# Each transfer by index waits for the last but one before it to land: sort, layers 0, 2, 3 and last stage of a four-layer graph network

## What is computed

```python
# layer 0, two steps: gated messages
edge_feat = concat([h[src], h[dst]]); messages = mlp(edge_feat) * sigmoid(mlp_att(edge_feat))
h = mlp(concat([h, segment_sum(messages, dst)])) + h + global_repr
# layer 1: segment_sum(x[col], row), then linear, batch norm, relu, linear
# layer 2: typed attention, 8 heads
attn = einsum('ehd,ehd->eh', Q[edge_dst], K[edge_src]) * rel_scale[edge_rel] / sqrt(DH)
out = segment_sum(softmax_over_dst(attn)[..., None] * V[edge_src], edge_dst) @ Wo + bo + skip
# layer 3: scores from q[src], k[tgt], edge attributes, distances; softmax over tgt
attended = weights[..., None] * v[tgt]; out = segment_sum(attended, tgt) @ Wo + bo
```

## Time and profile before

| | us |
|---|---|
| median of three timed runs (lowest, highest) | 7089.4 (7088.25, 7090.32) |
| span of the profiled execution | 8961.2 |
| its mean granted TensorE clock, share of full speed | 0.674 |
| PE busy in it | 5673.7 |
| DVE busy in it | 4867.9 |
| POOL busy in it | 4865.9 |

### The profile page before, as it was taken

One profiled execution on the slowest core, in us unless ns is written; L12 is line 12 of the kernel. 1 busy time (PEld: TensorE's weight loads), 2 busy tenths in 40 slices (PEclk: granted clock), 3 DMA queues, 4 the chain that ended last, 5 costly groups with the idle time before them and its releaser, 6 DMA issues. The chain is left out here.

```text
span 8961.2 us, 134318 instructions
## 1 busy us (share of the span) xinstructions
PE 5673.7 (63%) x28658; PEld 4800.1 (54%) x28659; DVE 4867.9 (54%) x17338; ACT 1151.3 (13%) x3238; POOL 4865.9 (54%) x4715
## 2 busy tenths in 40 slices
PE   6555556677777767777768778656666665333334
PEld 5555555466666556666655555456666663333333
DVE  6555554455555545555557777545555553444555
ACT  1111111111111111111112222100000001000001
POOL 2566564555555355555527888445454451566664
PEclk6555555777777877777779999865655556555556
DMA  5334434333333233333324444333333332333332
GB/s 154 95 95 97 94 94 126 92 97 93 95 93 96 57 102 94 94 97 98 94 53 67 69 69 69 78 83 88 89 89 87 89 89 37 77 75 75 74 77 49
DMA packets 930244, 770.85 MB, mean 86 GB/s; under 512 B 586631, under 2 KB 762899, under 8 KB 928115
## 3 DMA queue, kind: packets, MB, share of 16 engines
q0 software_dynamic: 245936, 426.87, 19.9%
q1 hardware_dynamic: 675276, 329.60, 14.6%
q10 hardware_dynamic: 8960, 13.52, 0.6%
HBM read 681.88 MB, written 86.32 MB: 86 GB/s over the span
## 5 line engine op out<-in xcount | busy, mean ns | idle before, releaser
L1180 POOL DMA_INDIRECT there<-table_wide,idx x1664 | 1597.4, 960 | 1396.8 <-DVE prod L1203 615.9
L1271 PE MATMUL ps<-here,hot_t 128*128 x3328 | 1238.1, 507 | 631.3 <-DVE there L1222 599.7
L2288 POOL DMA_INDIRECT there<-table_wide,idx x832 | 792.7, 953 | 902.6 <-DVE msg L2364 434.8
L1222 DVE TENSOR_TENSOR there<-there,ps 128x512 f32<-128x512 f32 x832 | 571.2, 687 | 1169.8 <-remote 607.7
L1271 PEld LDWEIGHTS ps<-here,hot_t 128*128 128x128 f32 x3328 | 740.9, 247 | 756.5 <-issue 668.9
L2677 POOL DMA_INDIRECT there<-table_narrow,idx x832 | 791.3, 951 | 649.5 <-issue 259.1
L693 POOL DMA_INDIRECT rec<-out_recd,posd x806 | 817.5, 1014 | 564.4 <-issue 263.9
L1279 PE MATMUL ps<-relu,hot_s 128*128 128x128 f32 x3328 | 878.0, 356 | 140.3 <-DVE hot_s L1211 108.1
L2837 PE MATMUL ps<-here,hot_t 128*128 x1664 | 434.5, 436 | 803.6 <-DVE prod L2758 419.3
L1947 POOL DMA_INDIRECT partial_sums<-row_sums1a,idx1a x504 | 814.9, 1617 | 167.4 <-issue 147.3
L1279 PEld LDWEIGHTS ps<-relu,hot_s 128*128 128x128 f32 x3328 | 688.5, 238 | 326.3 <-issue 272.1
(11 more groups left out here) (486 smaller groups left out, 9773.3 us busy)
## 6 DMA issues: line engine op xcount, KB each, us to landing
locrows<-loc_row SPq DMA_DIRECT2D x416, 256.0 KB
krowd<-key_row SPq DMA_DIRECT2D x201, 256.0 KB
there<-table_wide,idx POOLq DMA_INDIRECT x2496
src_rows1a<-slot_src_row SPq DMA_DIRECT2D x42, 768.0 KB
lrowd<-lo_row SPq DMA_DIRECT2D x201, 128.0 KB
attr_raw<-in_edge_attr SPq DMA_DIRECT2D x201, 128.0 KB
there<-table_narrow,idx POOLq DMA_INDIRECT x832
rec<-out_recd,posd POOLq DMA_INDIRECT x806
```

The source lines that it names most:

```text
L1180: nc.gpsimd.indirect_dma_start(there[:, j, q, :], None, table, bass.IndirectOffsetOnAxis(idx[:, j, q:q + 1], 0)).then_inc(gathered[j][q], 16)
L1222: nc.vector.tensor_tensor(pair, pair, ps[:, WORK, :], ALU.add).then_inc(summed, 1)
L1271: last = nc.tensor.matmul(ps[:, WORK, (q % 2) * 2 * F:(q % 2 + 1) * 2 * F], hot_t[:, j % 2, q * P:(q + 1) * P], here[:, :, :].rearrange("p ...
L2288: nc.gpsimd.indirect_dma_start(there[:, j, q, :], None, table, bass.IndirectOffsetOnAxis(idx[:, j, q:q + 1], 0)).then_inc(gathered[j][q], 16)
```

## The change

Before each gather or scatter by index, from the third on, Pool waits until the one two before it has landed, then increments `admitted`; after each group it waits for the landing of the group's last but one. At the second of a group the gathers of layers 0, 2 and 3 wait for the last of the group before. In the last stage the single semaphore `found` becomes two in turn, and DVE waits for both. Nothing is computed otherwise.

```diff
--- before.py
+++ after.py
@@ -690,8 +690,12 @@
                     pool.wait_ge(kept, i * 4 + (j + 3))
                     pool.sem_inc(admitted, 1)
                     for g in range(n):
+                        if g >= 2:
+                            pool.wait_ge(sent[j][g - 2], i * 16 + 16)
+                        pool.sem_inc(admitted, 1)
                         nc.gpsimd.indirect_dma_start(rec, bass.IndirectOffsetOnAxis(pos[:, j, g:g + 1], 0),
                                                      out[:, j, g, :], None).then_inc(sent[j][g], 16)
+                    pool.wait_ge(sent[j][n - 2], i * 16 + 16)
 
                 with pool.Fori(0, QUADS) as i:
                     for j in range(SLOTS):
@@ -1177,8 +1181,14 @@
                             pool.wait_ge(cut, i * RING * PR + (j * PR + q // 2 + 1))
                         pool.wait_ge(dotted, i * CH + (j * U + q + 1))
                         pool.sem_inc(admitted, 1)
+                        if q >= 2:
+                            pool.wait_ge(gathered[j][q - 2], i * 16 + 16)
+                        elif q == 1 and j:
+                            pool.wait_ge(gathered[j - 1][U - 1], i * 16 + 16)
+                        pool.sem_inc(admitted, 1)
                         nc.gpsimd.indirect_dma_start(there[:, j, q, :], None, table,
                                                      bass.IndirectOffsetOnAxis(idx[:, j, q:q + 1], 0)).then_inc(gathered[j][q], 16)
+                    pool.wait_ge(gathered[j][U - 2], i * 16 + 16)
 
         @block.vector
         def _(dve):
@@ -2920,10 +2942,11 @@
         turned, weight_kept, weight_made = c.sem("wo_turned"), c.sem("wo_kept"), c.sem("wo_centred")
         v_made, v_kept, moved, cen_made, cen_kept = c.sem("v_made"), c.sem("v_kept"), c.sem("h_moved"), c.sem("hc_made"), c.sem("hc_kept")
         ends_turned, line_step, lifted, spread = c.sem("ends_turned"), c.sem("line_steps"), c.sem("line_lifted"), c.sem("carry_spread")
-        found, node_step, node_lifted, massed = c.sem("runs_found"), c.sem("node_steps"), c.sem("node_lifted"), c.sem("massed")
+        node_step, node_lifted, massed = c.sem("node_steps"), c.sem("node_lifted"), c.sem("massed")
         weighed, agg_turned, agg_kept, projected = c.sem("weighed3"), c.sem("agg_turned3"), c.sem("agg_kept3"), c.sem("projected3")
         centred, squared, var_ready, rooted = c.sem("centred_last"), c.sem("squared_last"), c.sem("var_last"), c.sem("rooted_last")
         inverted, returned, normed, finished = c.sem("inverted_last"), c.sem("returned_last"), c.sem("normed_last"), c.sem("finished_last")
+        paced, founds = c.sem("paced_last"), [c.sem(f"runs_found{n}") for n in range(2)]
         out_turned, out_kept, stored = c.sem("out_turned3"), c.sem("out_kept3"), c.sem("out_stored")
         block = ctx.enter_context(nc.Block())
         SP = len(SPANS)
@@ -2932,8 +2955,12 @@
         @block.gpsimd
         def _(pool):
             for t in range(NB):
-                nc.gpsimd.indirect_dma_start(found_rows[:, t, :], None, spool, bass.IndirectOffsetOnAxis(run["pos"][:, t:t + 1], 0)).then_inc(found, 16)
-            pool.wait_ge(found, 16 * NB)
+                if t >= 2:
+                    pool.wait_ge(founds[t % 2], 16 * (t // 2))
+                pool.sem_inc(paced, 1)
+                nc.gpsimd.indirect_dma_start(found_rows[:, t, :], None, spool, bass.IndirectOffsetOnAxis(run["pos"][:, t:t + 1], 0)).then_inc(founds[t % 2], 16)
+            pool.wait_ge(founds[0], 16 * ((NB + 1) // 2))
+            pool.wait_ge(founds[1], 16 * (NB // 2))
 
         @block.tensor
         def _(pe):
@@ -3027,7 +3054,8 @@
             nc.vector.tensor_tensor(carried_in[:, 0, :, :], carried_in[:, 0, :, :],
                                     run["early"][:, :].rearrange("p (t o) -> p t o", o=1).to_broadcast([P, NB, H]), ALU.min).then_inc(node_step, 1)
             dve.wait_ge(node_step, 5)
-            dve.wait_ge(found, 16 * NB)
+            dve.wait_ge(founds[0], 16 * ((NB + 1) // 2))
+            dve.wait_ge(founds[1], 16 * (NB // 2))
             nc.vector.tensor_tensor(joint[:, :, :], found_rows[:, :, 0:H], carried_in[:, 0, :, :], ALU.max).then_inc(node_step, 1)
             dve.wait_ge(node_step, 6)
             nc.vector.tensor_tensor(scale[:, 0, :, :], found_rows[:, :, 0:H], joint[:, :, :], ALU.subtract).then_inc(node_step, 1)
```

## The result

| | before | after |
|---|---|---|
| median of 4 runs, us (lowest to highest) | 7088.82 (7069.89 to 7090.32) | 9705.5 (9686.01 to 9712.0) |
| span of the profiled execution shown, us | 8961.2 | 9699.9 |

The ratio is 1.3694, 95% interval 1.3672 to 1.3716: slower by 2617 us. Predicted were 8500 us, range 7230 to 8980. The sign was right; the size was not. (In experiment 3 one execution of four took 10761.6 us, at a granted clock of 1.0, where the others took 7627.66 to 7637.19; it is left out there.)

A forecast was written before the change was run, and what follows sets the result against it. The prediction took Pool's issue of index transfers as the bound: 4134 x 1.61 = 6656 us, layer 1 968.7, between layer 0's steps 120.0, the rest 747.0 and last stage 9 made 8501, so 8500 us; range 7230 to 8980.

The forecast's parts named there:

- Pool's issue bounds the timed kernel: All five stages with index transfers: Pool's issue, about 1.25 us a transfer back to back, sets the unprofiled pace; chance 0.74.
- Unprofiled, PE and DVE run faster: Reason given: without the profiler PE and DVE free slots in time, so some 1886 us of Pool's profiled idle time vanish.
- The agreement of 7075 with 7089: Sum of Pool's own pace (5239 us), layer 1, the time between layer 0's steps and the rest, against the measured median.
- everything shrinks without the profiler: Rival: the whole profile, Pool included, scales by 0.79 in timed runs, so the change costs about +140: 7230 us; chance 0.12.
- The instructions cost nothing: Added waits and increments on Pool are worked off during the 0.95 us of the transfer before, at no cost.
- D = 0.80 us: Time on Pool from a landing event to the start of the transfer that waited for it, read in layer 2.
- The wait is read ahead: Rival: a landing needs only 0.30 us to the next start, so the pace is 1.37 us, total 7502; chance 0.08.
- L = 2.43 us, with ends 2.2 and 2.65: Time from a transfer's start on Pool to its landing; gives a pace of 1.61 us, with ends 1.50 and 1.725.
- All other terms together: Forecast parts outside the paced transfers: layer 1 968.7 us, between layer 0's steps 120.0, the rest 747.0, last stage 9.
- Pairs and a pace, nothing hidden: Paced stages: interval is half of landing time plus restart delay; each stage lasts count x pace, ring depth hiding no pace.
- A gain by less traffic beside SP's loads: Rival: fewer gathers in flight speed SP's row loads in layers 0 and 2, some 30 to 50 us: 7050; chance 0.03.
- What would show it: Signs: Pool idle 0.5 to 0.8 us before transfers, starts two apart 3.1 to 3.5 us, busy 0.95, timed excess over 400.

The follow-up runs named there:

- experiment 3: The change's waits in layer 2 alone, against the kernel before on the same chip: 7631.14 us, ratio 1.0787.
- Experiment 0: The kernel before, unchanged, measured again on a chip other than that of the 8961.2 us profile: 7084.81 us, ratio 1.0012.
- experiment 1: Kernel before with as many added waits and increments in the sort and layers 0, 2, 3, each on an event long past: 7078.19 us, ratio 0.9999.
- experiment 4: Kernel before with each gather of layer 2 alone waiting for the landing of the one just before: 10477.46 us, ratio 1.169.
- 8: The changed kernel against the kernel before, both on a chip where the latter takes about 8975 us: 9653.51 us, ratio 1.0767.
- experiment 2: Kernel before with each transfer in the sort and layers 0, 2, 3 waiting for the landing of the fourth before it: 7131.45 us, ratio 1.0082.
- experiment 6: Layer 2 paced at two and SP's row-number loads there cut to an eighth, against the kernel before: 8945.27 us, ratio 0.9968.
- experiment 11: Kernel before with each transfer in the sort and layers 0, 2, 3 waiting for the third before it: 8734.01 us, ratio 0.9746.

## Why the prediction was right, and where it failed

- **Pool's issue bounds the timed kernel: right.** Experiment 0 shows the intervals that were computed (1.25 us back to back) and idle time of 0.30 us times the count. **The reason given for it was wrong.** "Unprofiled, PE and DVE run faster" has no ground; the profile shown was of a chip on which they are held up. The agreement of 7075 with 7089 was no accident (the stretches of experiment 0 make 5395 us where 5359 were counted, the rest 1683 where 1716 were), but it said what the bound was, not why the profile differed. The rival *everything shrinks without the profiler* falls with its premise.
- **The instructions cost nothing: right** (experiment 1).
- **D = 0.80 us: nearly right.** The chain of the changed kernel has 0.75; in its events the median is 0.77 in the three gather stages, and the mean, which counts, 0.89 to 0.91. *The wait is read ahead*, at 0.30, is refuted.
- **L = 2.43 us, with ends 2.2 and 2.65: this step failed.** The view of one line of the changed kernel (its median the middle number) and the page's list of DMA issues (median to landing last) have

```profile
DMA to landing us min/median/max: 2.6/2.8/4.9
```

```profile
there<-table_wide,idx POOLq DMA_INDIRECT x2496, 2.8
there<-table_narrow,idx POOLq DMA_INDIRECT x832, 2.5
rec<-out_recd,posd POOLq DMA_INDIRECT x806, 3.1
```

  The shortest landing of layer 2 (first fence, L2303) is 2.6 us, above the value taken. Its mean, by the events, is 3.06, with 2.95 in layer 0, 2.93 in layer 3 and 2.95 in the sort. Two errors make it up. The lower bound of 2.2 was the end of the bytes, read in the earlier trace rows, and the event comes later than they do: 0.35 us in the median over the gathers of experiment 4. And the upper bound of 2.65 was one landing, the last of the run, in a stage whose own landings are shorter: 2.22 to 2.38 us in most of the chain above. A single row was taken for a mean, while the load after the eighth gather had shown 3.19 and was set aside.
- **What it was worth.** The four stages (layer 0 without the 120 us between its steps) last 1515.0 + 3174.8 + 1640.9 + 1593.3 = 7924 us, that is 1.917 a transfer where 1.61 was taken: +1268 us. All other terms together came out 69 us lower than forecast. L + D is 3.83 on the mean instead of 3.23; some 0.5 of the difference is L, the rest D. With 2.95 and 0.88 in the same sum the forecast would have been 4134 x 1.915 + 1845 = 9762.
- **Pairs and a pace, nothing hidden: right.** Experiments 3, 4 and 8 show the interval as (L + D) / 2 in the gather stages, on both kinds of chip, and on A the growth of the four stretches adds up to that of the span within 27 us. In the sort the prediction's own remark counts: no transfer waits for the fourth scatter of a group, which lands latest (3.68 us in the mean, the other three 2.54 to 2.81), so starts two apart are 3.76 us, less than the mean L and D of all would give (4.04).
- **A gain by less traffic beside SP's loads: not on A** (experiment 2 is slower), and seven eighths of the row loads are worth 0.03 us a gather (experiment 6).
- **What would show it.** Idle time ended by its own DMA: yes, but 0.95 to 1.04 us a gather in place of 0.5 to 0.8. Starts two apart: 3.5 to 4.1 in the timeline, 3.8 to 4.0 in the mean, in place of 3.1 to 3.5. Busy 0.955 in layer 0 as foreseen, 1.02 in layer 2. A profiled span of 9000 to 9400: 9699.9 and, on the kind of chip for which it was meant, 9639.7.
- **The Trainium skill**, "DMA: Bandwidth & Descriptors", section "Anatomy of one DMA — SWDGE (gpsimd) path", gives 2.3 us for a transfer of 128 KB, an estimate by that page: for the wide gathers of the changed kernel 0.5 below the median of 2.8, and 0.6 to 0.8 below the mean that counts here. The section "Latency and other measured facts" has the fixed cost fall with a lighter load of HBM; with seven eighths of the row loads gone the median landing of layer 2 is 2.9 us against 3.0 on the same chip (26 landings each), the way the page says, but too small and on too few landings to bear it out.

## What to carry to other kernels

When a queue is limited to n transfers in flight, its pace is (time to landing + time from the event to the next start) / n, and it must be compared with the pace at which the engine issues: here 3.83 / 2 = 1.92 against 1.25 us, while at four the limit costs 0.8%. Take the time to landing as a mean over many transfers of that very stage, from engine start to event, never from the end of the bytes or from one transfer, and look which transfers of a group are late and whether anything waits for them: half a microsecond in it was over 1000 us here. And where a profiled span and the timed runs differ by a fifth, first ask whether they come from the same chip; the bound itself may be another engine's there, and the same edit cost 37% on one chip and 8% on another.

## What was not expected of the hardware

- The same program takes 7079, 8975, 9115 and 9112 us on four chips, each time repeated within 1%; on the slower kind results of PE reach DVE and ACT late in the sort and layer 0, unless transfers by index are held to two in flight.
- In layer 0 the granted clock of TensorE fell from 0.95 to 0.76 when Pool was paced, and in layer 2 from 0.70 to 0.62, in stretches where PE now stood idle more. It cost nothing, since PE was not the bound, but it hides what PE could do.
- Limiting the transfers in flight to three made the kernel 2.6% faster on the chips where PE's completions come late. In layer 2 alone it gave 1.5%. How three in flight help there is not settled: the label "remote" ends as much idle time as before (table above), and of the 241 us between the spans of the earlier trace rows and experiment 11, 127 lie in layer 2, 59 in layer 0, 29 in the sort and 21 in layer 3.
